# Adder layer 1's convolution as 64x64 quadrants, with layer 0's sums turned to natural channel order ahead of it

## The reference

```
def _adder3x3(x, w):
    ...                       # patches: [N, H, W, 64*9]
    def per_co(wc):
        return -jnp.sum(jnp.abs(patches - wc), axis=-1)
...
out = _adder3x3(_conv3x3(x, conv1_w, stride=1), add1_w)
out = jax.nn.relu(_bn_train(out, bn1_g, bn1_b))
out = _adder3x3(_conv3x3(out, conv2_w, stride=1), add2_w)
out = _bn_train(out, bn2_g, bn2_b)
return jax.nn.relu(out + x)
```

## Time and profile before

| | us |
|---|---|
| median of 3 runs | 3963.75 |
| fastest, slowest run | 3952.57, 3967.20 |
| the profiled execution: time | 3959.45 |
| the profiled execution: span of its core | 3957.70 |
| PE, DVE, ACT, POOL busy | 3311.5, 3075.9, 2901.6, 909.0 |
| layer 0 of the adder: conv starts, adder loop ends | 618.1, 1629.6 |
| layer 1: conv starts, adder loop ends | 1642.4, 2671.5 |
| first instruction of the sampler phase (last block) | 2698.85 |

### The profile page before, as it was taken

One profiled execution on the slowest core, in us unless ns is written; L12 is line 12 of the kernel. 1 busy time (PEld: TensorE's weight loads), 2 busy tenths in 40 slices (PEclk: granted clock), 3 DMA queues, 4 the chain that ended last, 5 costly groups with the idle time before them and its releaser, 6 DMA issues. The chain is left out here.

```text
span 3957.7 us, 58571 instructions
## 1 busy us (share of the span) xinstructions
PE 3311.5 (84%) x22186; PEld 1315.6 (33%) x22186; DVE 3075.9 (78%) x3332; ACT 2901.6 (73%) x2954; POOL 909.0 (23%) x974
## 2 busy tenths in 40 slices
PE   3788648999999999899999999997686787786666
PEld 2455414233333333332333334433232232232212
DVE  5777666999999999579999999993376666666555
ACT  1767523999999999479999999991356665656655
POOL 1100000000000000000000000000577777777775
PEclk7666578999999999999999999998798897898677
DMA  2200000000000000000000000000213123123211
GB/s 47 103 1 1 1 0 4 1 2 2 1 1 1 2 2 1 1 1 2 1 1 1 1 2 1 2 1 16 55 53 74 53 58 74 53 62 70 58 53 43
DMA packets 117620, 89.55 MB, mean 23 GB/s; under 512 B 96496, under 2 KB 98576, under 8 KB 117340
## 3 DMA queue, kind: packets, MB, share of 16 engines
q0 software_dynamic: 28672, 58.78, 5.3%
q1 hardware_dynamic: 87036, 26.30, 3.0%
q10 hardware_dynamic: 1632, 0.56, 0.1%
HBM read 65.60 MB, written 19.96 MB: 22 GB/s over the span
## 5 line engine op out<-in xcount | busy, mean ns | idle before, releaser
L1579 ACT ACTIVATE adder_layer_Z<-adder_layer_CP,AN 128x2048 f32 x984 | 1873.3, 2005 | 31.4 <-PE PS L1540 30.5
L1540 PE MATMUL PS<-adder_layer_Z,c_adder_out 128*32 128x512 f32 x16896 | 1843.2, 593 | 57.6 <-ACT adder_layer_Z L1579 32.5
L1625 DVE TENSOR_SCALAR adder_layer_Z<-adder_layer_CP,AW 128x2048 f32 x1128 | 1369.7, 1281 | 44.8 <-PE PS L1540 30.7
L1540 PEld LDWEIGHTS PS<-adder_layer_Z,c_adder_out 128*32 128x32 f32 x16896 | 645.4, 110 | 1255.1 <-issue 1180.8
L1996 POOL DMA_INDIRECT sampler_G<-neighbours,sampler_IDX x896 | 853.4, 952 | 373.7 <-issue 272.9
L2283 ACT ACTIVATE sampler_HY<-PS,G_hat 128x512 f32<-128x512 f32 x512 | 308.9, 685 | 266.3 <-PE PS L2162 205.4
L1632 DVE SCALAR_TENSOR_TENSOR adder_layer_Z<-adder_layer_CP,AW,adder_layer_Z 128x1024 f32<-128x1024 f32 x384 | 476.4, 1282 | 33.5 <-issue 33.5
L2055 DVE TENSOR_TENSOR sampler_G<-sampler_G,PS 128x1792 f32<-128x1792 f32 x64 | 129.4, 2021 | 157.9 <-DMA sampler_G<-neighbours,sampler_IDX 152.7
L2285 ACT ACTIVATE sampler_HY<-sampler_HY 128x2048 f32<-128x2048 f32 x128 | 244.5, 1910 | 9.0 <-issue 0.4
L1497 POOL MEMSET XP<- 128x4624 f32 x1 | 4.0, 3952 | 1044.2 <-PE PS L1556 1044.2
L1492 POOL MEMSET adder_layer_CP<- 128x4624 f32 x2 | 7.9, 3954 | 1020.0 <-POOLq L1487 1019.8
(11 more groups left out here) (380 smaller groups left out, 2862.6 us busy)
## 6 DMA issues: line engine op xcount, KB each, us to landing
sampler_G<-neighbours,sampler_IDX POOLq DMA_INDIRECT x896
neighbours<-top_k_zero SPq DMA_DIRECT2D x16, 578.0 KB, 7.0
neighbours<-sampler_HT SPq DMA_DIRECT2D x256, 32.0 KB, 1.7
X<-in_x SPq DMA_DIRECT2D x8, 256.0 KB, 6.2
out<-X SPq DMA_DIRECT2D x8, 256.0 KB, 3.1
P<-in_L_conv_conv_w SPq DMA_DIRECT2D x4, 144.0 KB
P<-in_L_conv_add_w SPq DMA_DIRECT2D x4, 144.0 KB
RAW<-in_L_conv_w SPq DMA_DIRECT2D x4, 144.0 KB
```

The lines of the kernel that those rows point to most:

```text
L1540: mm = t.matmul(PS[32 * j:32 * j + 32, k, :], K["adder_out"][:, 32 * i:32 * i + 32], Z[:, r % SLOTS, j, c:c + BANK], start=False, stop=Fal ...
L1579: op = a.activation(z(r, j), seen(ch, ty, tx), ACT.Relu, bias=ANf[:, weight(ty, tx, j, i)])
L1625: op = v.tensor_scalar(z(r, j), seen(ch, ty, taps[0]), AWf[:, weight(ty, taps[0], j, i)], 0.0, ALU.subtract, ALU.max)
```

## The change: what it does

Layer 1's convolution takes the form of layer 0's: four quadrants, two banks at a time, `BANKS` order. A quadrant needs each half's channels on its own 64 partitions, so layer 0 must hand its result over in natural order. For that, layer 0 gets the matmuls by `to_nat`: banks 1 to 7 as soon as their sums are copied (before the matmuls of the statistics), then the scale and the bias as two matmuls with one column (their result lies in bank 0), and last bank 0. ACT copies the turned scale and bias to a new small tile, `natural`, and its four final instructions read PSUM where they read `SO` before. Their order is now pair 1, 2, 3, 0. The weights of layer 1's convolution are loaded in natural order (a plain copy of the same form as the others) and masked by `half_nat`.

```diff
@@ load, weights @@
-                            if q == 2:
-                                load(RAW1[:, q, :, :].rearrange("o (j h i) t -> o j h (i t)", j=NJ, h=2)[:, :, h],
-                                     w.rearrange("o (j i) t -> o j (i t)", i=NI))
-                            else:
-                                load(RAW1[:, q, 64 * h:64 * h + 64, :], w)
+                            load(RAW1[:, q, 64 * h:64 * h + 64, :], w)
...
-                            block_weights(v, WC[i], ps9, "half_perm" if q else "half_nat")
+                            block_weights(v, WC[i], ps9, "half_nat")
@@ adder_layer @@
-                BANKS = [0, 2, 1, 3, 4, 6, 5, 7] if layer == 0 else list(range(NBANK))
+                BANKS = [0, 2, 1, 3, 4, 6, 5, 7]
+                natural = sb("natural", [128, 2])
@@ PE, convolution: layer 0's form for both layers @@
-                        else:
-                            for k in range(NBANK):
-                                for tap in range(TAPS):
-                                    mm = t.matmul(bank(k), WC[1][:, tap, :], patch(src, k, tap), start=(tap == 0),
-                                                  stop=(tap == TAPS - 1))
-                                mm.then_inc(c_ps, 1)
+                            for tap in range(TAPS):
+                                for i in range(2):
+                                    k = BANKS[n + i]
+                                    for h in range(HALVES):
+                                        r, o = 64 * h, 64 * (h ^ i)
+                                        mm = t.matmul(PS[o:o + 64, k, :], WC[layer][r:r + 64, tap, r:r + 64],
+                                                      patch(src, k, tap)[r:r + 64], start=(tap == 0),
+                                                      stop=(tap == TAPS - 1), skip_group_check=True)
+                            mm.then_inc(c_ps, 2)
@@ PE, after the adder loop @@
+                        def to_natural(k):
+
+                            for h in range(HALVES):
+                                o = 64 * (h ^ (k // 2 % 2))
+                                mm = t.matmul(PS[o:o + 64, k, :], K["to_nat"][:, 64 * h:64 * h + 64],
+                                              SO[:, BANK * k:BANK * k + BANK], start=True, stop=True,
+                                              skip_group_check=True)
+                            mm.then_inc(nat_ps, 1)
+
+                        if not layer:
+                            for k in range(1, NBANK):
+                                t.wait_ge(s_sb, k + 1)
+                                to_natural(k)
                         gn.pe(t, 1, K["mean_pair"][:, :])
+                        t.wait_ge(normed, 1)
                         if layer:
-                            t.wait_ge(normed, 1)
                             for k in range(NBANK):
...
+                                to_natural(k)
+                        else:
+                            t.matmul(PS[:, 0, 128:129], K["to_nat"][:, :], gn.scale[:, 0:1], start=True, stop=True)
+                            t.matmul(PS[:, 0, 129:130], K["to_nat"][:, :], gn.bias[:, 0:1], start=True,
+                                     stop=True).then_inc(nat_ps, 1)
+                            t.wait_ge(border, 1)
+                            to_natural(0)
@@ ACT, end of layer 0 @@
-                            a.wait_ge(normed, 1)
-                            for b in range(NB):
+                            a.wait_ge(nat_ps, NBANK)
+                            a.activation(natural[:, :], PS[:, 0, 128:130], ACT.Copy)
+                            a.drain().then_inc(border, 1)
+                            for b in (1, 2, 3, 0):
+                                if b == 0:
+                                    a.wait_ge(nat_ps, NBANK + 1)
                                 a.activation(P2[:, b, 1:H + 1, 1:W + 1],
-                                             SO[:, PX * b:PX * b + PX].rearrange("p (y x) -> p y x", y=H), ACT.Relu,
-                                             scale=gn.scale[:, 0:1], bias=gn.bias[:, 0:1])
+                                             PS[:, 2 * b:2 * b + 2, :].rearrange("p a (y x) -> p (a y) x", x=W),
+                                             ACT.Relu, scale=natural[:, 0:1], bias=natural[:, 1:2])
```

More of the change, by code:

```diff
@@ L1503, in _ @@
                             t.sem_inc(z_free[slot], 1)
-                        if layer == 0:
-                            for n in range(0, NBANK, 2):
+                        for n in range(0, NBANK, 2):
+                            if quantiser:
                                 quantiser.pe_before(t, n)
                                 quantiser.pe_before(t, n + 1)
-                                for tap in range(TAPS):
-                                    for i in range(2):
-                                        k = BANKS[n + i]
-                                        for h in range(HALVES):
-                                            r, o = 64 * h, 64 * (h ^ i)
-                                            mm = t.matmul(PS[o:o + 64, k, :], WC[0][r:r + 64, tap, r:r + 64],
-                                                          patch(src, k, tap)[r:r + 64], start=(tap == 0),
-                                                          stop=(tap == TAPS - 1), skip_group_check=True)
-                                mm.then_inc(c_ps, 2)
-                        else:
-                            for k in range(NBANK):
-                                for tap in range(TAPS):
-                                    mm = t.matmul(bank(k), WC[1][:, tap, :], patch(src, k, tap), start=(tap == 0),
-                                                  stop=(tap == TAPS - 1))
-                                mm.then_inc(c_ps, 1)
+                            for tap in range(TAPS):
[7 more added lines that the diff above has]
+                            mm.then_inc(c_ps, 2)
                         t.wait_ge(ready, 1)
@@ L1549, in _ @@
                             mm.then_inc(s_ps, 1)
+                        def to_natural(k):
[9 more added lines that the diff above has]
+                                to_natural(k)
                         gn.pe(t, 1, K["mean_pair"][:, :])
+                        t.wait_ge(normed, 1)
                         if layer:
-                            t.wait_ge(normed, 1)
                             for k in range(NBANK):
-                                for h in range(HALVES):
-                                    o = 64 * (h ^ (k // 2 % 2))
-                                    mm = t.matmul(PS[o:o + 64, k, :], K["to_nat"][:, 64 * h:64 * h + 64],
-                                                  SO[:, BANK * k:BANK * k + BANK], start=True, stop=True,
-                                                  skip_group_check=True)
-                                mm.then_inc(nat_ps, 1)
+                                to_natural(k)
[5 more added lines that the diff above has]
+                            to_natural(0)
                     @blk.scalar
```

## The result

| | before | after |
|---|---|---|
| median, us | 3953.9 (5 runs) | 3933.09 (5 runs) |
| fastest, slowest | 3952.36, 3967.20 | 3929.68, 3937.62 |
| profiled execution: time, span | 3959.45, 3957.7 | 3929.68, 3927.9 |

The ratio is 0.9941, with a 95% interval from 0.9929 to 0.9953: 0.59 percent faster, 18.6 to 28.1 us of 3953.9. The forecast was 0.55 percent, 21.75 us.

The account below looks back on a forecast made before the run. It took the stretch between the layers' loop ends as decisive, with PE, DVE and ACT all busy in the loops. -25.35 - 0.2 + 2.3 + 1.5 = -21.75 us on the median 3963.75 gave 3942.0, range 3928 to 3955.

Parts of the forecast that it names:

- What bounds the kernel: Adder layers: barriers move the last block as a whole, so layer 0's loop end to layer 1's loop end counts.
- The convolution: Layer 1's conv: 33.63 us to the last two copies' start instead of 64.32, 30.7 us less, not all arriving.
- The third box sum, exposed: Layer 1 after the conv: DVE's first map 40.04 us after the conv's start, against 65.39, a gain of 25.35.
- The loop: Layer 1 from DVE's first map to PE's final box-sum matmuls: ACT's lead of 4.9 us gains 0.2 (bounds 0 and 0.46).
- The hand-over: Layer 0's end: 2.3 us for the first statistics matmul queued behind seven banks' turning, 1.5 for turning scale and bias.
- the chain behind the bias: Layer 0's end, bias to ACT's relu: two small matmuls and ACT's copy add 1.5 us (bounds 1.1 and 1.8).
- The sum: Whole change: -25.35 - 0.2 + 2.3 + 1.5 = -21.75 us, or -0.55 percent on the median.
- The signs: Profile after, both layers and last block: stretch lengths and start times that would show the forecast right or wrong.
- The absolute time: Whole kernel: 3942.0 us, from the three runs' median of 3963.75 and the forecast change of -21.75.
- ACT-paced: Layer 1's loop: ACT sets its end, so ACT's earlier start counts; -26.4 us, a median of 3937; chance 0.10.
- The dearer hand-over: Layer 0's end: PE's clock falls, 14 matmuls take 12 us, not 6; -15.5 us, median 3948; chance 0.08.
- No overlap: Layer 1's conv: quadrants take turns, a pair of banks takes 15.5 us; kernel 9.3 us slower, 3973; chance 0.04.

Follow-up runs that it names:

- the late box sum: Changed kernel with layer 1's third box sum moved from ahead of the loop to between its chunks; ratio to the kernel before 0.9925.
- the run in which ACT waits: Changed kernel with ACT starting layer 1's maps only when the third box sum is done; chunk 1 took 478.19 us, single run.

## Why the prediction was right, point by point

- **What bounds the kernel.** The chain of waits says nothing of these layers; loop end to loop end is what counts. Right: the total moved as that stretch did, 21.46 us, within its interval of 18.6 to 28.1.
- **The convolution**, 33.63 us to the last copies from layer 0's rows: 33.69. Right, and the stated 7.73 for a pair too. Shown alone by the run with the conv only.
- **The third box sum, exposed**: DVE's first map at 40.04, measured 40.15. Right. The gain is 25.24 (25.35 forecast), not 30.6. That DVE's start and not ACT's sets the chunk's end is shown by the late box sum (without the lag the chunk ended 6.1 us earlier, ACT starting as before) and by the run in which ACT waits (5 us later, the same end).
- **The loop**, 959.8 forecast, 961.05 measured, outside its bounds of 959.5 to 960. I had taken layer 0 as a guide, where ACT leads as well, and asked only what the lead gives (0.2). What I passed over is that PE there works through the wait on the quantiser's matmuls (1.42 us idle), and here stands idle for 6.61. The term was +1.06 in place of -0.2. The half clock is the cause of 0.9 of it, shown by the two runs with extra matmuls; the rest comes at the turns. The lead itself gave nothing: with five extra matmuls, the same lead and the clock at 1.00 the loop took 960.08, against 959.99 before.
- **The hand-over**, +3.8 forecast (2.3 + 1.5), +2.72 measured. The queue ahead of the statistics was right (6.02 us after the loop's end forecast, 6.10 measured). The step mis-sized is the chain behind the bias, +1.5 forecast with bounds from 1.1: it was +0.93 (1635.66 less 1634.61 is 1.05, less the old 0.12). I took a small matmul's time from rows at the half clock, 0.58, and put 1.13 for two of them; after the turning PE is at full clock, they take 0.38 each, the second starts 0.25 behind the first, and ACT's copy begins 0.65 after the first. The same made the statistics 0.4 us shorter, so the first part was +2.02. The relus from PSUM took 4.50 against 4.64, and the phase change was 0.1 shorter.
- **The sum.** -25.24 + 1.06 + 2.72 = -21.46, against -21.75. That it is so close is luck: the loop was 1.26 us worse than forecast and the hand-over 1.08 better, and these nearly cancel.
- **The signs.** Three of those that the prediction named did not come: the loop of 959.5 to 960 (961.05), the 3.5 to 4 us more between the loop's end and the conv (2.72), and an unchanged time from layer 1's loop end to the span's end (4.2 us less). The last is also one of its signs of being wrong; I put it down to scatter, since the last block alone runs from 1253.7 to 1258.8 in profiles that all do the same work there, but what makes it vary stays open.
- **The absolute time**, 3942.0, lies 9 us over the median of 3933.09. The anchor was high: the three runs shown had a median of 3963.75, all five of before have 3953.9, and the medians of before measured beside the experiments were 3958.0 (21 runs), 3959.0 (11) and 3955.7 (9).
- **Rivals.** ACT-paced: refuted in what it forecast, that ACT's earlier start would count; that ACT is the engine without gaps inside a turn was right, but its lead stops at the slots. The dearer hand-over: refuted, clock and distance of the turning stayed (28 records in 6.23 us). No overlap: refuted in layer 1 as in layer 0, 72 records of four quadrants in 7.73 us. The rule on PSUM banks that the prediction cites from the Trainium skill ("TensorEngine Tiling (Array Packing)", section "Restrictions and Gotchas"), that different row tiles cannot access one bank at the same time, does not hold here, where two row tiles write different partitions of the same bank.

## What to carry to other kernels

When a stage gets shorter, list what lay under it. Here a box sum had hidden under the conv and came out behind it, at 5 of the 31 us; moving it to a place where its engine waited anyway gave them back and 1.2 us more. Matmuls put ahead of a small one that a chain waits for delay the chain by their whole length, even where PE had been idle; put them behind it, into the waits one by one (2.4 of 2.7 us back). And take a duration from a row in which the engine had the same past: the two terms that missed both came from rows at another clock. Last, an engine that is early is not yet an engine with room: ACT's five microseconds of lead gave nothing, and 0.9 us that it lost at the start stayed lost, because from there on it had no gap.

## What I had not expected of the hardware

- The loop's turn: with 10 or 12 more matmul records (five or six matmuls of two passes) ahead of a loop on PE, a pause at its turn moved from behind 14 records to behind 4 and 2, that is by exactly that number. Behind 14 records it was 0.7 to 1.4 us long, behind 4 it was 1.6 to 2.3, behind 2 it was 2.2 and 2.3. In the kernel before and with the conv alone none shows in chunk 1, and the kernel before has one behind 4 records in chunk 2. Pauses up to 1.9 us cost the chunk 0.2 us at most; those from 2.0 on cost 0.4 to 3.1 each. The place in the instruction stream and an instruction transfer that ends 1.2 to 1.6 us before PE goes on speak for a wait for instructions. No run that moves the transfer alone shows it, and that queue 8 is PE's is my reading.
- One box sum more on DVE's path between the chunks cost nothing, but two box sums on the idle POOL cost 14.4 us, because each of DVE's maps beside them took 3.0 us instead of 1.2.
- The stretches of a loop of 960 us repeat to 0.2 us in most profiles, so edits worth 1 us can be judged there, while whole executions scatter by 8 to 15 us.
